# Flamingo block, one core: context projections of the second attention behind the experts, routing first on all engines, second attention reordered

## Chip, core and metric

One core of one Trainium2 chip. The engines are TensorE (PE in the profile), VectorE (DVE), ScalarE (ACT), GpSimd (POOL) and SyncE (SP, which issues the transfers). The metric is the device time of one execution in microseconds.

## What is computed

32 sequences of 64 tokens with 128 features go through two layers; each adds a gated attention over a context and a gated feed-forward part:

```python
x = x + tanh(g_xattn[0]) * attention(layernorm(x), ctx)       # softmax, 16 heads, rotary
x = x + tanh(g_ffn[0])   * experts(layernorm(x))              # 2 of 8 experts per sequence
x = x + tanh(g_xattn[1]) * autocorrelation(layernorm(x), ctx) # below
x = x + tanh(g_ffn[1])   * fp4_ffn(layernorm(x))              # gate/up 352 wide, SiLU, down
# autocorrelation, per sequence and head:
corr = irfft(rfft(Q) * conj(rfft(K))).mean(-1); w, idx = top_k(corr, 4); w = softmax(w)
out = sum_k w[k] * roll(V, idx[k]) @ Wo + bo
```

The router takes the mean of a sequence's tokens, picks the two best of eight logits, and weighs both experts' outputs with a softmax. `fp4_ffn` rounds its inputs and weights in blocks of 16 to an eight-value grid.

## The kernel before

Every engine has its own instruction list in an order written out by hand; semaphores (`m[...]`) join them, and each engine works its list strictly in order. The tokens are 16 tiles of 128 x 128 (two sequences each), in four groups. `ps` is PSUM with eight banks of 512 columns; a step may not overwrite a bank before its reader has gone.

- **First attention** (to about 99 us): 16 tiles, one after the other.
- **Routing** (99 to 120.4). `pool_tokens` (L1165) sums the normalised tokens on PE into bank 0, DVE copies them (`pooled`, L759), PE forms the logits (L1182), and DVE and PE take turns: best two, membership `mem`, ranks, `tcol`, `tend`, slots (L761 to L797). `experts` (L791) releases SP, whose `feed` copies each expert's weights from `wall` into one of six `wbuf`; `packed` (L806) releases POOL, whose `gather` (L380) copies the chosen sequences out of `xt`. Meanwhile PE turns the tokens (`turn_tokens`, L1034), takes the context to frequencies (`context_to_frequency`, L1143) and projects it (`context_kv`, L1159, eight steps of 512 columns: four for K, four for V). ACT copies each K and V step out of PSUM twice: plain (`kf`, `vf`, L532) and with real and imaginary halves exchanged (`kfs`, `vfs`, L534). DVE fills `acc` with the experts' second bias (L809, 2048 columns), adds biases to the zero frequency of K and V (L819), and PE waits for `acc_ready` ahead of the first expert.
- **Experts**: 36 tiles of two slots. `hidden(j)` (L1214), GELU on ACT (L542), `second(j)` (L1223), `collect` on DVE adds into `acc`. POOL also prepares the fp4 weights.
- **Second attention**: `turn_weights` (L1241, L1245) and its copies, then PE turns `acc` back (L1254), DVE adds it to `x` and takes statistics (`moe_out`), POOL raises to a power (`powers`), ACT normalises (L239). `to_frequency` (L1262), `queries` (L1269), a bias on DVE (L871), `products` with K (L874), `sum_heads` (L1283), `correlate` (L1293, L1299), `best_lags` (L880 to L896, with ACT's `exp_lead`), `turn_lags`, `turn_gx` (L581), `spectrum` (L1329), `roll_values` (L904), POOL's `values_added` (L408), `out_product` (L1336), `y1_turned`, `out_tokens` (L1343), and DVE's `attention_out` (L932) with `x_stats`.
- **fp4 part**: per group of four tiles `x_scale` (L265 to L272), `x_magnitude` on ACT, `x_round` (L276), `x_unscale` on POOL (L283), `turn_x` (L1369), `turned_x` (L614). Per pair of tiles `gate_up` (L1379), `silu` (L619) and `pair_step` on DVE, which begins with the product of L957, then `turn_h` and `down`. Groups 2 and 3 are scaled and rounded inside the loop over pairs.

## Time and profile before

| | us |
|---|---|
| median of 3 runs (311.04 to 312.18) | 312.07 |
| profiled execution | 312.27 |
| its span, first to last instruction | 310.5 |
| PE busy | 260.1 |
| DVE busy | 205.5 |
| ACT busy | 163.6 |
| POOL busy | 114.7 |
| mean granted clock of PE, 1 is full | 0.943 |

The span is what the trace shows; 1.77 us of the profiled execution lie around it. Busy time is an average over the stages above, and in each of them another engine or chain sets the end, so it is to be read by stretch. In a timeline, a number in brackets is the idle time of the engine ahead of the row, with what ended it; "x8" means eight instructions in a row.

### The profile page before, as it was taken

To read this page: it belongs to the slowest core of one execution; us is meant where nothing else is said; L and a number is where in the kernel's file an instruction comes from. 1 tells how busy PE (TensorE), PEld (TensorE's weight loads), DVE (VectorE), ACT (ScalarE), POOL (GpSimd) and SP (SyncE) were. 2 spreads that over 40 slices of the span, in tenths; PEclk is the share of its full clock that TensorE was granted. 3 is DMA by queue.
4 is the path that set the end of the run, shared out by engine and by line. 5 is a ranking of instruction groups with operands and counts; after the bars stand their busy time and mean duration, and the time that the engine had idled before them with its cause. 6 is when DMAs were issued, how large, how long until landed. Compare 5 with 4: busy or idle time off the path is not lost.

```text
span 310.5 us, 6172 instructions
## 1 busy us (share of the span) xinstructions
PE 260.1 (84%) x2126; PEld 199.1 (64%) x2126; DVE 205.5 (66%) x556; ACT 163.6 (53%) x381; POOL 114.7 (37%) x163
## 2 busy tenths in 40 slices
PE   2999889999898988999999994987892857598675
PEld 1565257666667935999999993666661424467474
DVE  3499988888986355342322337663989499999951
ACT  1169365666584578775566553762327352434321
POOL 3174549993202103229952202300554303231230
PEclk9999999999999999999999999699997588979957
DMA  7994000000000208676777710000000000001011
GB/s 246 357 387 196 0 3 2 2 2 0 3 2 2 74 2 364 262 303 276 292 291 305 291 70 3 1 0 2 0 0 1 0 2 0 0 17 34 19 34 35
DMA packets 11871, 30.13 MB, mean 97 GB/s; under 512 B 961, under 2 KB 5057, under 8 KB 11713
## 3 DMA queue, kind: packets, MB, share of 16 engines
q1 hardware_dynamic: 11840, 29.75, 25.2%
q8 instruction: 17, 0.28, 0.4%
q14 instruction: 14, 0.11, 0.1%
HBM read 9.75 MB, written 1.05 MB: 35 GB/s over the span
## 4 chain that ended last, share of the span: by engine, by line
PE 53%; DVE 30%; ACT 7%; issue 5%; DMA 3%; POOL 1%; SPq 0%; DVEq 0%
PE ps L1223 10%; PE ps L1214 9%; PE ps L1104 5%; DVE s_region L276 4%; PE ps L1078 4%; PE ps L1091 4%; DVE s_small L225 3%; DVE s_region L680 3%; PE ps L1401 2%; DVE s_small L967 2%; DVE s_region L272 2%; PE ps L1114 2%; PE ps L1283 2%; DMA s_region<-s_wall 2%; PE ps L1379 2%
## 5 line engine op out<-in xcount | busy, mean ns | idle before, releaser
L542 ACT ACTIVATE s_region<-ps,s_region 128x128 f32<-128x128 f32 x144 | 40.8, 371 | 20.5 <-PE ps L1214 20.4
L834 DVE SCALAR_TENSOR_TENSOR s_ctxT<-ps,s_region,s_ctxT 128x64 f32 x72 | 18.1, 281 | 45.7 <-PE ps L1223 45.4
L1214 PE MATMUL ps<-s_region 128*128 128x128 f32 x288 | 37.9, 276 | 0.8 <-DVE s_ctxT L810 0.5
L1223 PE MATMUL ps<-s_region 128*128 128x128 f32 x288 | 38.0, 276 | 0.5 <-ACT s_region L542 0.5
L1214 PEld LDWEIGHTS ps<-s_region 128*128 128x128 f32 x288 | 34.9, 192 | 1.8 <-DVE s_ctxT L810 1.3
L1223 PEld LDWEIGHTS ps<-s_region 128*128 128x128 f32 x288 | 35.0, 192 | 0.9 <-ACT s_region L542 0.7
L1379 PE MATMUL ps<-s_region 128*128 128x352 f32 x64 | 25.9, 558 | 11.3 <-DVE s_region L957 6.1
L283 POOL TENSOR_TENSOR s_region<-s_region,s_small 128x704 f32<-128x704 f32 (+2 forms) x13 | 17.5, 1343 | 47.6 <-DVE s_region L276 47.6
L248 POOL TENSOR_TENSOR s_small<-s_small,s_par 128x4 f32<-128x4 f32 (+3 forms) x14 | 15.5, 1108 | 47.1 <-DVE s_small L231 47.1
L380 POOL COPY s_region<-s_xt 128x64 f32 x72 | 14.9, 240 | 40.2 <-PE ps L1214 21.9
L490 ACT COPY s_region<-ps 128x512 f32<-128x512 f32 x32 | 17.2, 589 | 18.2 <-PE ps L1091 18.2
L1379 PEld LDWEIGHTS ps<-s_region 128*128 128x128 f32 x64 | 13.8, 227 | 20.2 <-issue 10.3
L338 POOL TENSOR_SCALAR s_region<-s_region 128x512 f32<-128x512 f32 x16 | 24.7, 1567 | 3.7 <-PE ps L1078 3.7
L701 DVE TENSOR_REDUCE s_small<-ps 128x16 f32<-128x1024 f32 x16 | 19.6, 1222 | 6.5 <-PE ps L1078 6.5
L239 ACT ACTIVATE s_xn<-s_x,s_small 128x128 f32<-128x128 f32 x48 | 19.9, 485 | 6.9 <-POOL s_small L250 6.8
L276 DVE SCALAR_TENSOR_TENSOR s_region<-s_region 128x704 f32<-128x704 f32 (+1 forms) x24 | 20.3, 848 | 2.2 <-ACT s_region L625 0.9
L1401 PE MATMUL ps<-s_region 128*128 128x128 f32 (+1 forms) x96 | 15.6, 324 | 5.9 <-DVE s_x L979 4.1
L1401 PEld LDWEIGHTS ps<-s_region 128*128 128x128 f32 (+1 forms) x96 | 14.6, 234 | 9.0 <-issue 5.9
L485 ACT ACTIVATE s_region<-s_region 128x1024 f32<-128x1024 f32 x16 | 17.1, 1069 | 6.2 <-DVE s_region L709 6.2
L709 DVE TENSOR_TENSOR s_region<-ps,s_small 128x1024 f32<-128x1024 f32 x16 | 18.7, 1171 | 0.1
L1104 PEld LDWEIGHTS ps<-s_region 128*64 128x64 f32 x512 | 16.3, 138 | 3.5 <-ACT s_region L490 1.9
L1104 PE MATMUL ps<-s_region 128*64 128x18 f32 x512 | 17.8, 212 | 0.7 <-ACT s_region L490 0.6
(205 smaller groups left out, 507.0 us busy)
## 6 DMA issues: line engine op xcount, KB each, us to landing
s_region<-s_wall SPq DMA_DIRECT2D x36, 514.0 KB, 3.2
s_wall<-wall SPq DMA_DIRECT2D x8, 514.0 KB, 9.2
s_par<-par SPq DMA_DIRECT2D x1, 1316.0 KB, 11.1
s_ctxT<-ctxT SPq DMA_DIRECT2D x2, 512.0 KB, 6.0
s_x<-x SPq DMA_DIRECT2D x2, 512.0 KB, 7.4
out<-s_x SPq DMA_DIRECT2D x8, 128.0 KB, 1.8
s_region<-ffn SPq DMA_DIRECT2D x1, 560.0 KB, 3.6
s_par<-par SPq DMA_DIRECT2D x1, 460.0 KB, 3.8
```

The lines of the kernel that those rows point to most:

```text
L239: ins = eng.activation(xn[:, t, :], x[:, t, :], ACT.Identity, bias=shift[:, t:t + 1], scale=rstd[:, t:t + 1])
L276: return eng.scalar_tensor_tensor(out, mag, 1.5, z, ALU.max, ALU.subtract)
L338: pool.tensor_scalar(kbd[g % 2][:, j, :], cols, hmask[:, j:j + 1], None, ALU.mult).then_inc(m["kbd_done"], 1)
L542: ins = act.activation(hg[j % 3][:, c, :], ps[:, j % 3, RPT * S * c:RPT * S * (c + 1)], ACT.Gelu, bias=wbuf[j % 6][:, FF + FC * D + c:FF + ...
L701: dve.tensor_reduce(mx[t % 2], scores(t % 2), AX, ALU.max).then_inc(m["mx_done"], 1)
L709: dve.tensor_tensor(ssub[t % 2], scores(t % 2), mx[t % 2].unsqueeze(2).broadcast_to([P, H, S]), ALU.subtract).then_inc(m["s_sub"], 1)
L834: dve.scalar_tensor_tensor(row, ps[:, 4 + j % 2, S * k:S * k + S], w, row, ALU.mult, ALU.add).then_inc(m["acc_done"], 1)
L1104: ins = mm(ps[S * row:S * row + S, 6 + t % 2, n * c:n * c + n], pT[t % 2][:, c, S * row:S * row + S], vbd[:, 2 * t + row, c, :], start=Tru ...
L1214: ins = mm(ps[:, j % 3, RPT * S * c:RPT * S * (c + 1)], w[:, P * c:P * c + P], xg[j % 4], start=True, stop=True)
L1223: ins = mm(ps[:, 4 + j % 2, 0:RPT * S], w[:, FF + D * c:FF + D * c + D], hg[j % 3][:, c, :], start=(c == 0), stop=(c == FC - 1))
L1379: ins = mm(ps[:, 1 + 2 * n + t % 2, 0:MLP], xqT[(t // 4) % 2][:, P * (t % 4):P * (t % 4) + P], wguT[:, MT * P * n:MT * P * n + MLP], start ...
L1401: ins = mm(ps[:, 7, D * t:D * t + D], hT[q % 2][0:n, t, k, :], wdT[0:n, k, :], start=(k == 0), stop=(k == MT - 1))
```

## The change

The exchanged copies `kfs` and `vfs` go; DVE reads `kf` and `vf` with the two halves in reverse order. The biases of Q, K and V are added on PE, by a product of the identity with eight columns of bias into the same bank (`frequency_bias`). During routing PE does routing steps ahead of everything else, and only `context_to_frequency(0)` to `(2)` stay ahead of the experts; `context_to_frequency(3)` and all eight `context_kv` move behind them, and so does `turn_weights`, to the middle of the second attention. ACT instead of DVE fills `acc`, POOL clears its spare rows at the start. The order of the second attention changes on every engine, the last two groups are normalised by DVE, `x_round(1)` moves into the loop over pairs, and the first `gate_up` waits for the value products, not for the last attention output. The core of the diff:

```diff
...
-        kf, kfs, vf, vfs = (carve(2048 * i, B, 2, DFT) for i in range(4))
+        kf, vf = carve(0, B, 2, DFT), carve(4096, B, 2, DFT)
...
+            for q in range(4):
+                values_added(q)
+            powers(pool, 0, 4)
+            values_added(4)
+            values_added(5)
             powers(pool, 4, 8)
+            values_added(6)
+            values_added(7)
+            x_unscale(0)
...
-            x_unscale(0)
...
+                if q in (2, 4):
+                    x_unscale(q // 2 + 1)
...
+                act.copy(ctxF[:, 512 * g:512 * g + 512], ps[:, 3 if g == 3 else 4 + g % 2, :]).then_inc(m["cf_used"], 1)
...
-            tokens_turned(0)
...
+                z, bank = (kf, 6 + n % 2) if n < G4 else (vf, 2 + n % 2)
+                act.copy(z[:, 8 * (n % G4):8 * (n % G4) + 8].rearrange("p b c s -> p (b c s)"), ps[:, bank, :]).then_inc(m["kv_used"], 1)
...
+            for g in range(3):
+                tokens_turned(g)
...
             act.activation(le[0:B], ld[0:B], ACT.Exp).then_inc(m["le_ready"], 1)
...
-                plain, swapped = (kf, kfs) if g < G4 else (vf, vfs)
-                src = ps[:, 6 + g % 2, :].rearrange("p (b c s) -> p b c s", c=2, s=DFT)
-                act.copy(plain[:, rows], src)
-                for c in range(2):
-                    ins = act.copy(swapped[:, rows, 1 - c], src[:, :, c])
-                ins.then_inc(m["kv_used"], 1)
+            tokens_turned(3)
+            context_turned(0)
+            context_turned(1)
+            context_turned(2)
+            act.wait_ge(m["b2_done"], 1)
+            act.copy(acc[:, 0:B, :], ps[:, 2, 0:B].unsqueeze(2).broadcast_to([P, B, S])).then_inc(m["acc_ready"], 1)
...
+            preload(ACT.Exp)
...
+            kv_turned(0)
+            context_turned(3)
+            kv_turned(1)
             normalise(act, 0, 4, m["xn_c"], 7)
+            kv_turned(2)
+            x_turned(0)
             normalise(act, 4, 8, m["xn_c"], 8)
-            x_turned(0)
-            normalise(act, 8, 12, m["xn_c"], 9)
+            kv_turned(3)
+            q_turned(0)
             x_turned(1)
-            q_turned(0)
-            normalise(act, 12, 16, m["xn_c"], 10)
             x_turned(2)
             q_turned(1)
...
             x_turned(3)
-            q_turned(2)
+            heads_turned(0)
             q_turned(3)
-            preload(ACT.Exp)
-            heads_turned(0)
             exp_lead(0)
             heads_turned(1)
+            kv_turned(4)
             turn_gx(0)
+            kv_turned(5)
             exp_lead(1)
+            preload(ACT.Silu)
...
+            kv_turned(6)
+            kv_turned(7)
+            weights_turned(0)
+            weights_turned(1)
             y1_turned(0)
+            weights_turned(2)
...
@@ -630,30 +640,27 @@
                     act.wait_ge(m["xd_done"], g - 1)
                 act.activation(qm[g % 2], qv[g % 2], ACT.Abs, scale=FINE).then_inc(m["xm_done"], 1)
 
...
-            normalise(act, 0, 4, m["xn_d"], 11)
-            y1_turned(3)
             normalise(act, 4, 8, m["xn_d"], 12)
             x_magnitude(0)
-            preload(ACT.Silu)
+            y1_turned(3)
+            turned_x(0)
             normalise(act, 8, 12, m["xn_d"], 13)
-            turned_x(0)
...
             x_magnitude(1)
-            silu(0)
             normalise(act, 12, 16, m["xn_d"], 14)
-            turned_x(1)
             for q in range(PAIRS + 1):
-                g = q // 2 + 2
...
-                if q in (2, 4):
+                if q in (0, 2, 4):
                     turned_x(q // 2 + 1)
 
...
-            normalise(dve, 8, 12, m["xn_b_late"], 4)
+                if t == 14:
+                    normalise(dve, 8, 12, m["xn_b_late"], 4)
...
-            sr.did(dve.tensor_copy(lidf[0:B], lidx[0:B, 0:2]))
-            sr.step(dve.tensor_tensor(ld[0:B], lmax[0:B, 1:2], lmax[0:B, 0:1], ALU.subtract))
-            dve.sem_inc(m["ld_ready"], 1)
+            sr.step(dve.tensor_copy(lidf[0:B], lidx[0:B, 0:2]))
             for k in range(2):
                 sr.did(dve.tensor_scalar(oh[0:B, k, :], pc("iota_e", B), lidf[0:B, k:k + 1], None, ALU.is_equal))
             sr.settle()
+            dve.tensor_tensor(mem[0:B], oh[0:B, 0, :], oh[0:B, 1, :], ALU.add).then_inc(m["route_in"], 1)
+            dve.tensor_tensor(ld[0:B], lmax[0:B, 1:2], lmax[0:B, 0:1], ALU.subtract).then_inc(m["ld_ready"], 1)
...
+            dve.tensor_tensor(ohb[0:B], ohs[0:B, 0, :], ohs[0:B, 1, :], ALU.add).then_inc(m["route_in"], 1)
...
-            dve.tensor_copy(acc[:, 0:B, :], ps[:, 2, 0:B].unsqueeze(2).broadcast_to([P, B, S])).then_inc(m["acc_ready"], 1)
...
+            sr.did(dve.tensor_scalar(wt[0:B], oh[0:B, 0, :], lw[0:B, 0:1], None, ALU.mult))
+            sr.step(dve.tensor_scalar(ohw[0:B], ohs[0:B, 0, :], lw[0:B, 0:1], None, ALU.mult))
+            dve.scalar_tensor_tensor(wt[0:B], oh[0:B, 1, :], lw[0:B, 1:2], wt[0:B], ALU.mult, ALU.add).then_inc(m["wt_ready"], 1)
+            dve.scalar_tensor_tensor(ohw[0:B], ohs[0:B, 1, :], lw[0:B, 1:2], ohw[0:B], ALU.mult, ALU.add).then_inc(m["wt_ready"], 1)
+            dve.wait_ge(m["wt_turned"], 1)
+            dve.tensor_copy(wtT[0:E], ps[0:E, 3, P:P + B]).then_inc(m["wt_copied"], 1)
+            dve.wait_ge(m["wt_turned"], 2)
+            dve.tensor_copy(wB, ps[:, 1, 0:SLOTS]).then_inc(m["weights_spread"], 1)
+            dve.wait_ge(m["weights_spread"], 1)
+            dve.wait_ge(m["spare_zero"], 2)
+            dve.wait_ge(m["acc_ready"], 1)
...
-                    dve.tensor_scalar(z[:, :, c, 0], z[:, :, c, 0], b64[:, 1 + n:2 + n], None, ALU.add).then_inc(m["kv_biased"], 1)
...
-                dc.step(dve.tensor_scalar(qf[:, rows, 0, 0], qf[:, rows, 0, 0], b64[:, 0:1], None, ALU.add))
...
+                for z, k in ((pp, kf[:, rows]), (pq, kf[:, rows, ::-1, :])):
+                    dve.tensor_tensor(z[:, rows], qf[:, rows], k, ALU.mult).then_inc(m["pp_done"], 1)
...
+                for z, (o, v) in enumerate(((of1, vf[:, rows]), (of2, vf[:, rows, ::-1, :]))):
...
+            normalise(dve, 8, 12, m["xn_c_late"], 9)
+            products(0)
+            normalise(dve, 12, 16, m["xn_c_late"], 10)
+            products(1)
             dve.tensor_scalar(bo1g, pc("bo1"), tg[:, 2:3], None, ALU.mult).then_inc(m["bo_scaled"], 1)
-            for g in range(G4):
-                products(g)
+            products(2)
+            products(3)
...
-                bias_added(q)
-            roll_values(4)
...
+            bias_added(0)
+            bias_added(1)
+            out_and_stats(0)
+            roll_values(4)
             roll_values(5)
-            out_and_stats(0)
+            out_and_stats(1)
+            x_scale(0)
             roll_values(6)
             roll_values(7)
-            out_and_stats(1)
+            x_round(0)
+            bias_added(2)
             out_and_stats(2)
-            x_scale(0)
-            attention_out(3)
-            x_round(0)
-            x_stats(3)
+            bias_added(3)
+            out_and_stats(3)
             x_scale(1)
-            x_round(1)
...
+                if q in (0, 2, 4):
+                    x_round(q // 2 + 1)
+                if q in (1, 3):
+                    x_scale((q + 3) // 2)
...
+                if t == TILES - 1:
+                    pool_tokens(0, 2)
                 weigh_values(t)
                 if t >= 1:
                     project_out(t - 1)
+            pool_tokens(2, 3)
             turn_output(TILES - 1)
+            pool_tokens(3, 4)
...
+            def frequency_bias(bank, n):
+
+                pe.wait_ge(m["bias64_ready"], 1)
+                out = ps[:, bank, :].rearrange("p (b c s) -> p b c s", c=2, s=DFT)[:, :, 0, 0]
+                return mm(out, ident, b64[:, n, :], start=False, stop=True)
...
+                pe.wait_ge(m["cf_used"], n + 1 if n < G4 else G4)
+                bank = 6 + n % 2 if n < G4 else 2 + n % 2
+                if n < 2:
+                    pe.wait_ge(m["tr2_used"], n + 3)
+                elif n < G4 or n >= G4 + 2:
                     pe.wait_ge(m["kv_used"], n - 1)
+                elif n == G4:
+                    pe.wait_ge(m["xf_used"], G4)
                 else:
-                    pe.wait_ge(m["tr2_used"], n + 3)
-                mm(ps[:, 6 + n % 2, :], pc("wk1" if n < G4 else "wv1"), ctxF[:, 512 * (n % G4):512 * (n % G4) + 512],
-                   start=True, stop=True).then_inc(m["kv_done"], 1)
-
...
+                mm(ps[:, bank, :], pc("wk1" if n < G4 else "wv1"), ctxF[:, 512 * (n % G4):512 * (n % G4) + 512], start=True, stop=False)
+                frequency_bias(bank, 1 + n // G4).then_inc(m["kv_done"], 1)
...
+            pool_tokens(4, 12)
...
+            pool_tokens(12, TILES).then_inc(m["pool_sums"], 1)
             pe.wait_ge(m["pooled_ready"], 1)
             mm(ps[0:B, 1, 0:E], pooled, pc("wr"), start=True, stop=True).then_inc(m["route_mm"], 1)
-            context_kv(0)
-            context_kv(1)
-            context_kv(2)
+            turn_tokens(1)
+            turn_tokens(2)
...
+            turn_tokens(3)
...
+            context_to_frequency(0)
...
+            context_to_frequency(1)
+            pe.wait_ge(m["wt_ready"], 1)
+            tr(ps[0:E, 3, P:P + B], wt[0:B], pc("ident", B)[:, 0:B]).then_inc(m["wt_turned"], 1)
+            pe.wait_ge(m["wt_ready"], 2)
+            mm(ps[:, 1, 0:SLOTS], pc("ones", B), ohw[0:B], start=True, stop=True).then_inc(m["wt_turned"], 1)
+            context_to_frequency(2)
+            pe.wait_ge(m["wt_copied"], 1)
+            mm(ps[:, 2, 0:B], pc("b2", E), wtT[0:E], start=True, stop=True).then_inc(m["b2_done"], 1)
...
+                elif j >= 1:
+                    pe.wait_ge(*((m["weights_spread"], 1) if j == 1 else (m["acc_ready"], 1)))
...
+                pe.wait_ge(m["wq_ready"], 1)
+                pe.wait_ge(*((m["wq_used"], 1) if g == 2 else (m["kv_used"], 7 + g)))
...
+                frequency_bias(2 * (g % 2) + 1, 0).then_inc(m["q_done"], 1)
...
+                pe.wait_ge(m["kv_used"], G4)
...
+            context_kv(0)
+            turn_experts(0)
+            turn_experts(1)
+            context_to_frequency(3)
+            context_kv(1)
+            turn_experts(2)
+            context_kv(2)
+            turn_experts(3)
             to_frequency(0)
+            context_kv(3)
+            queries(0)
             to_frequency(1)
-            queries(0)
             to_frequency(2)
             queries(1)
+            sum_heads(0)
+            queries(2)
             to_frequency(3)
-            queries(2)
-            sum_heads(0)
+            sum_heads(1)
             queries(3)
-            sum_heads(1)
             correlate(0)
             sum_heads(2)
             sum_heads(3)
+            context_kv(4)
...
             turn_lags(0)
             spectrum(0)
+            context_kv(5)
             spectrum(1)
             turn_lags(1)
             spectrum(2)
+            context_kv(6)
             spectrum(3)
+            context_kv(7)
+            turn_weights(0)
+            turn_weights(1)
             out_product(0)
+            turn_weights(2)
             spectrum(4)
+            spectrum(5)
             out_tokens(0)
-            spectrum(5)
             out_product(1)
+            out_tokens(1)
             spectrum(6)
-            out_tokens(1)
             spectrum(7)
-            for g in range(2, G4):
-                out_product(g)
-                out_tokens(g)
+            out_product(2)
+            out_tokens(2)
+            out_product(3)
+            out_tokens(3)
...
+                    pe.wait_ge(m["of_done"], 2 * PAIRS)
+                    pe.wait_ge(m["wq_used"], 3)
+                    if t == 1:
+                        pe.wait_ge(m["y1_ready"], G4)
...
+                else:
+                    pe.wait_ge(m["x3_done"], G4)
...
-            turn_x(1)
...
-                if q in (2, 4):
+                if q in (0, 2, 4):
                     turn_x(q // 2 + 1)
...
```

## Rows read from the trace of the kernel before

**Rows 1.** Busy time by stretch (us, then PE, PEld, DVE, ACT, POOL, PEclk, DMA).
```profile
99.00:120.40 21.40, 18.96 (x117) 12.53 (x115) 12.00 (x58) 12.85 (x31) 2.50 (x7) 1.00 0.26 96
120.40:186.70 66.30, 65.35 (x578) 64.84 (x579) 20.39 (x78) 43.99 (x150) 29.14 (x76) 1.00 0.66 266
186.70:199.00 12.30, 8.07 (x42) 6.39 (x41) 9.34 (x47) 7.25 (x17) 4.75 (x8) 0.75 0.00 1
```

**Rows 2.** Timeline of DVE, 101 to 120: start, us, line, operation, idle before.
```profile
101.74 1.29 DVE L241 TENSOR_SCALAR s_xn<-s_x,s_small 128x128 f32<-128x128 f32 x4
106.59 0.19 DVE L759 COPY s_small<-ps 128x32 f32<-128x32 f32 x1 [3.56 <-PE ps L1165]
108.18 0.15 DVE L761 TENSOR_SCALAR s_small<-ps 32x8 f32<-32x8 f32 x1 [1.40 <-PE ps L1182]
...
112.12 0.15 DVE L779 COPY s_small<-ps 32x8 f32<-32x8 f32 x1 [1.45 <-PE ps L1190]
...
114.36 0.18 DVE L791 TENSOR_SCALAR s_small<-ps 1x36 int32<-1x36 f32 x1 [0.56 <-PE ps L1196]
...
116.55 0.22 DVE L799 SCALAR_TENSOR_TENSOR s_small<-ps,s_par 1x72 f32<-1x72 f32 x1 [0.93 <-PE ps L1201]
...
117.93 2.27 DVE L809 COPY s_ctxT<-ps 128x2048 f32<-128x2048 f32 x1
```

**Rows 3.** Timeline of PE, 99 to 113.
```profile
99.92 1.85 PE L1165 MATMUL ps<-s_par,s_xn 128*128 128x2 f32 x16
...
110.67 1.10 PE L1159 MATMUL ps<-s_region,s_par 128*128 128x512 f32 x2 [0.46 <-ACT s_region L534]
```

**Rows 4.** Timeline of ACT, 121 to 127.
```profile
121.17 1.28 ACT L437 ACT_TABLE_LOAD   x1
...
122.70 4.42 ACT L542 ACTIVATE s_region<-ps,s_region 128x128 f32<-128x128 f32 x16
```

**Rows 5.** Timeline of POOL, 102 to 120.
```profile
119.49 0.24 POOL L380 COPY s_region<-s_xt 128x64 f32 x1 [16.85 <-issue]
```

**Rows 6.** Timeline of PE, from the end of the experts.
```profile
186.51 0.82 PE L1241 MATMUL ps<-s_par,s_region 128*128 128x128 f32 x6
...
187.95 1.04 PE L1254 MATMUL ps<-s_par,s_ctxT 128*128 128x128 f32 x8
...
194.13 2.08 PE L1262 MATMUL ps<-s_par,s_xn 128*128 128x128 f32 x8 [1.76 <-ACT s_xn L239]
...
242.66 5.00 PE L1379 MATMUL ps<-s_region 128*128 128x352 f32 x8 [0.67 <-ACT s_region L614]
...
249.53 2.60 PE L1379 MATMUL ps<-s_region 128*128 128x352 f32 x8 [1.42 <-DVE s_region L957]
...
270.13 3.88 PE L1379 MATMUL ps<-s_region 128*128 128x352 f32 x8 [3.56 <-ACT s_region L614]
```

**Rows 7.** Timeline of ACT, 218 to 224.
```profile
222.74 1.01 ACT L581 COPY s_region<-ps 128x1024 f32<-128x1024 f32 x1 [4.64 <-PE ps L1329]
```

**Rows 8.** Timeline of DVE, 219 to 287.
```profile
219.39 0.75 DVE L904 TENSOR_TENSOR s_region<-ps,s_region 128x256 f32<-128x256 f32 x2
...
227.44 0.74 DVE L932 SCALAR_TENSOR_TENSOR s_x<-ps,s_small,s_x 128x512 f32<-128x512 f32 x1
...
229.68 1.47 DVE L904 TENSOR_TENSOR s_region<-ps,s_region 128x256 f32<-128x256 f32 x4
...
235.55 0.68 DVE L265 TENSOR_REDUCE s_small<-s_xn 128x32 f32<-128x512 f32 x1
...
238.26 1.42 DVE L276 SCALAR_TENSOR_TENSOR s_region<-s_region 128x512 f32<-128x512 f32 x2
...
248.49 0.89 DVE L957 TENSOR_TENSOR s_region<-s_region,ps 128x704 f32<-128x704 f32 x1 [3.30 <-ACT s_region L619]
...
280.63 0.88 DVE L957 TENSOR_TENSOR s_region<-s_region,ps 128x704 f32<-128x704 f32 x1
...
286.23 0.89 DVE L957 TENSOR_TENSOR s_region<-s_region,ps 128x704 f32<-128x704 f32 x1
```

183 lines of the change are left out of this document (64 added, 119 removed).

## Prediction

> **What bounds the kernel now.** I read the page first, then busy time by stretch, then each engine's timeline around the stretches that the change touches. Four limits follow each other. From 99 to 120.4 no engine is full: PE, ACT and DVE pass the routing result back and forth, with context work queued between the steps [rows 1]. From 120.4 to 186.7 PE is busy 65.35 of 66.30 us [rows 1]: the experts are PE's, nothing is gained inside them, and what counts is when they start. From 186.7 PE waits for DVE's statistics and its granted clock averages 0.75 [rows 1], half speed at 194 [rows 6]. From about 219 DVE sets the pace: its groups carry no idle time except 3.30 us before the first product of the pair loop at 248.49 [rows 8]; later one pair step takes 286.23 - 280.63 = 5.60 us [rows 8].
>
> Times below are on the clock of the trace of before. The sum is made against the profiled execution, 312.27 us (span 310.5 and 1.77 around it), 0.2 above the median of 312.07.
>
> **Part 1: routing first.** Before, the last token tiles are normalised from 101.74 to 103.03 [rows 2] and their sums reach DVE at 106.59, behind two `context_to_frequency` and two `turn_tokens`. Now `normalise(dve, 8, 12)` runs in DVE's idle time in tile 14, so the last tile is ready about 1.0 earlier, at 102.05; four of the sixteen pooled tiles go into attention's gaps (a tile costs 1.85 / 8 = 0.23 of PE [rows 3]), and one is left when the last normalise ends. The sums are read at 102.5, 4.1 earlier.
> - L759 to L761: 1.59 [rows 2], of it 1.40 waiting for PE behind context work; now about 0.5. Gain so far 5.2.
> - L761 to L779: 3.94, with 1.45 of waiting behind `context_kv(2)` and the softmax weights in line. Now 1.4 of arithmetic to `mem` and 0.35 for two small matmuls: 104.7, gain 7.4.
> - L779 to L791: 2.24; the wait of 0.56 behind `context_kv(3)` and the copy of `wtT` go: 106.3, gain 8.1. `experts_ready` and the weight transfers move with it.
> - L791 to L799: 2.19; two operations on `ohw` and most of the 0.93 wait go: 107.45, gain 9.1.
> The codes are packed 1.3 later (108.8), and POOL's first row copy, at 119.49 before [rows 5], comes at 110.4. Expert 0's first matmuls can start at 111.2.
>
> Then ACT is late. It still has `context_turned(2)` (PE work of 0.9 queued ahead of the `b2` product, ends 111.45), then the broadcast into `acc`, formerly DVE's 2.27 [rows 2]. A broadcast copy of 1024 columns takes ACT 1.01 [rows 7]; 2048 columns I take at 1.9, to 113.4. The GELU table costs 122.70 - 121.17 = 1.53 [rows 4]: first GELU at 115.0 against 122.70. **Gain 7.7.** Behind ACT's new wait for `b2_done` stand the GELUs; PE's `hidden(1)` and `hidden(2)` wait for `weights_spread` (110.3) and `acc_ready` (113.4), both before `second(0)` could run. POOL's wait for `tr2_used` ends at 105.9, long before the codes. No transfer changes its place on SP. Low 6.2, if each of the eight hand-offs costs 0.2 more than I read; high 8.9, if the `acc` copy finished as early as the rest of the routing. The swapped copies on ACT and four bias additions on DVE lay in front of this point and are inside the gain.
> The Trainium skill (ScalarE: Activation LUTs, What ACT_TABLE_LOAD costs) puts every switch of tables at about 2.66 us, a drain behind the load included. This trace does not agree: the load lasts 1.28 and the next instructions follow at once [rows 4]; by the page the gain would be 6.6.
>
> **Part 2: front of the second attention.** After the experts the three turned weights (1.44 from 186.51 to 187.95 [rows 6]) give way to `context_kv(0)`: 512 columns, issue to issue 0.86 (a pair shows 1.10 with its tail [rows 3]), and a bias matmul of about 0.21. So the statistics start 0.4 earlier. The other context work, `context_to_frequency(3)` 0.9 and two `context_kv` 1.07 each, fills PE while it waited, so the clock should not fall at 193. A mean of 0.75 means that half of the 12.3 us were at half clock [rows 1]; eight 128-wide instructions take 1.04 at full and 2.08 at half [rows 6], so some 5.3 us of PE work from 194.1 shrink by 2.7. ACT's `preload(Exp)`, 1.5, leaves the path too. Against it stand `context_kv(3)` and `(4)`, 2.1, and four bias products, 0.8. I take the second correlation 2.0 earlier. Then the new order gives it back: ACT does `kv_turned(5)` before `exp_lead(1)`, and `context_kv(5)` stands behind `spectrum(0)` on PE. `exp_lead(1)` is ready at 215.7 and runs at 218.6, 2.9 late; DVE waits for it. `roll_values(0)` starts at 220.0 instead of 219.39 [rows 8].
>
> **Part 3: the output chain.** `spectrum(3)` has `context_kv(6)` in front, so `turn_gx(1)` starts at 223.85, before 222.74 [rows 7]. From there everything is in line: 1.0 for it; `kv_turned(6)` and `(7)` 1.1; then `turn_weights(1)` 0.35, `out_product(0)` 0.9, `turn_weights(2)` 0.35, `spectrum(4)` and `(5)` 1.7, `out_tokens(0)` 1.1: 230.4. DVE adds the first group at 230.4, before at 227.44 [rows 8]: **3.0 late**, with some 4.7 of DVE idle.
>
> DVE's queue to the pair loop, by rows 8: four outputs with statistics at 229.68 - 227.44 = 2.24; four value products at 1.38 / 2 (from 1.47 for two pairs); two scalings at 238.26 - 235.55 - 0.78 = 1.93; one rounding 1.34; two bias additions taken at 0.65 (below the 0.74 of an output of the same columns); 0.35 of waiting for ACT. Sum 8.96 + 2.76 + 3.86 + 1.34 + 1.30 + 0.35 = 18.6: first product of the pair loop at 249.0, against 248.49. The 3.30 that DVE idled there is thus what pays for the late output. `gate_up(0)` and `(1)` start at about 244.8; they took 5.00 at half clock, 2.60 for the next two at full clock [rows 6]. The first product followed the gates' start by 5.83 [rows 6, 8], so 0.83 goes to SiLU and hand-offs: 248.2 or 250.6, and the loop starts at 249.0 or 250.6. PE has gaps of up to 2.4 shortly before; I take 249.6: **1.1 lost** (0.5 to 2.1).
>
> **Part 4: the pair loop.** `x_round(1)` moves into it: **1.3 lost**. X tiles arrive one step later than before. From the end of a rounding, 239.68, to the first product made of it, 248.49, passed 8.8 at half clock [rows 8], 6.4 with gates at 2.60. After rounding 1 and 2 a step and a scaling, 7.4, cover it roughly; after rounding 3 one step of 5.6 alone. Half clock is likely there: the pair of gates at 270.13 came after 3.56 of idle and took 3.88 [rows 6]. That makes 7.6, and 2.0 late; full clock 0.8. **I take 1.2**, bounds 0 and 3.2.
>
> **Sum.** 312.27 - 7.7 + 1.1 + 1.3 + 1.2 = 308.2, less 0.2 for the median: **308.0**. Nearly half of the gain in routing is given back. Operands read with the halves reversed: no row has one; DVE's products are costed as plain ones (256 columns 0.37 [rows 8]), and the other bound, twice that, adds 3 over eight value products. I take nothing, since the runs of 32 numbers stay whole. The new memset on POOL stands before its first waits for DVE.
>
> **Rivals.**
> - **A, all of the gain stays (304 to 306.4).** Clock full at the first gates, no late tile, and the 2.0 of Part 2 kept in part: 312.1 - 7.7 + 0.5 + 1.3 = 306.2, less up to 2. For it: the 3.30 of idle. Against it: the order on ACT in Part 2. Chance 0.22.
> - **B, the pair loop waits at each new X tile (310.5 to 313.5).** Gates at 5.00 throughout: start at 250.6 (2.1), rounding 1.3, late by 0.8, 0.9 and 3.2: 8.3 lost, 312.7. For it: rows 6 show 5.00 and 3.88. Against: most groups of the loop start after short waits. Chance 0.15.
> - **C, half clock between 214 and 230 (above 313.5; slower).** PE's work on the path there, two spectra, three `context_kv`, turned weights, `out_product(0)`, `out_tokens(0)`, sums to about 8.4 at full clock and would double; all of Part 3 is in line, so `out_tokens(0)` ends near 238, and 308.0 becomes 316. It decides once 5 us of that PE work run at half clock. For it: the stop and go with ACT. Against: PE's gaps there are 1.5 at most, and 194.13 was at half clock after a longer quiet stretch [rows 6]. Chance 0.13.
> The Trainium skill (TensorE: Matmul & The Clock Gate, HAM oscillation) warns of this pattern: each wait that lets the clock fall makes the next group run cold, again and again. By it C gains weight; what rows 6 show at 194, 242 and 270 agrees.
> - **D, routing's head start does not reach the experts.** Weights arrive late or ACT's chain grows, and only 5 of 7.7 remain: 310.7. Against: the transfers are issued 8 earlier too. It overlaps B's times; chance 0.05.
> The forecast itself, 306.4 to 310.5, has 0.45.
>
> **Numbers.** A measurement of this kernel tells about 0.5%, 1.6 us, from no change. Faster by more: the forecast, A and 0.03 of D: 0.70; within: B and 0.02 of D, 0.17; slower: C, 0.13. The range takes in the forecast, nearly all of A, D and most of B, some 0.83: 304.5 to 312.5.
>
> **What would show it.** First GELU near 115.0, with `experts_ready` 8 earlier; PE's clock 1.0 between 187 and 200; ACT's exponent of the second half near 210.9 (218.6 less 7.7) with DVE waiting; first attention output near 222.7; first pair product near 242; a gap before the seventh. Wrong if the GELU gain is under 6, or if DVE does not idle before the first output.

## The result: slower, 317.9 us against 311.8

| | before | after |
|---|---|---|
| median of four runs each (lowest to highest), us | 311.81 (311.04 to 312.18) | 317.90 (316.69 to 319.68) |
| profiled execution, us | 312.27 | 318.17 |
| its span | 310.5 | 316.4 |
| mean granted clock of PE in it | 0.943 | 0.905 |

The ratio of after to before is 1.0176, 95% interval 1.0131 to 1.0222. Ratios, here and below, leave out the slower executions that some kernels have now and then, while medians are over all. Forecast were 308.0, with 304.5 to 312.5 as range. Read by way points, as lengths between them in the two profiled executions, the 5.9 us of the span lie so (the first is where the last tile of the first attention weighs its values on PE; the forecast column is worked out from the prediction's own clock times):

| stretch | before | after | difference | forecast |
|---|---|---|---|---|
| start to last attention tile | 96.22 | 95.63 | -0.59 | 0 |
| to the first GELU | 26.48 | 23.89 | -2.59 | -7.7 |
| experts, to DVE's first group added | 65.96 | 65.38 | -0.58 | 0 |
| to the first value product | 30.73 | 31.69 | +0.96 | +0.6 (with the row above) |
| to the first attention output | 8.05 | 10.63 | +2.58 | +2.4 |
| to the first product of the pair loop | 21.05 | 22.27 | +1.22 | -1.9 |
| to its last, eighth | 43.31 | 48.32 | +5.01 | +2.5 (with the row below) |
| to the end | 18.70 | 18.59 | -0.11 | |

The gain in routing is 5.1 smaller than forecast, the start of the pair loop 3.1 later, the loop 2.4 longer; the other rows came out within 0.6.

First the busy time by stretch of the changed kernel; the first three lines answer to [rows 1], the last two cut the first stretch in two.

```profile
99.00:120.40 21.40, 20.75 (x102) 18.43 (x102) 8.00 (x47) 8.41 (x15) 4.26 (x16) 0.52 0.45 175
120.40:186.70 66.30, 66.22 (x577) 64.78 (x576) 21.99 (x83) 43.61 (x147) 27.24 (x67) 1.00 0.59 240
186.70:199.00 12.30, 10.69 (x68) 8.13 (x67) 11.43 (x51) 7.59 (x17) 5.78 (x8) 1.00 0.01 2
...
99.00:109.00 10.00, 9.37 (x52) 8.35 (x52) 5.44 (x33) 2.44 (x5) 1.74 (x4) 0.51 0.18 57
109.00:120.40 11.40, 11.38 (x52) 10.08 (x52) 2.56 (x15) 5.97 (x10) 2.52 (x12) 0.53 0.69 278
```

The column after POOL is the granted clock. After the experts it went from 0.75 to 1.00, as forecast. In routing it went from 1.00 to 0.52, and that the prediction had not priced. PE had *less* work of routing there than before (the context projections are gone) and yet shows 20.75 us busy of 21.40, against 18.96. Part of that is the first experts' products, which now begin at 116.00; the rest is the same work at half speed.

PE's timeline of the changed kernel (line numbers are now its own: L1123 sums, L1156 context to frequency, L1365 output matmul, L1411 gates). Answers to [rows 3] and [rows 6].

```profile
98.44 2.67 PE L1123 MATMUL ps<-s_par,s_xn 128*128 128x2 f32 x16
...
101.86 1.71 PE L1123 MATMUL ps<-s_par,s_xn 128*128 128x2 f32 x8
...
113.43 2.08 PE L1156 MATMUL ps<-s_par,s_ctxN 128*128 128x128 f32 x8
...
190.38 1.16 PE L1273 MATMUL ps<-s_par,s_xn 128*128 128x128 f32 x8 [1.31 <-ACT s_xn L239]
...
237.27 1.16 PE L1358 MATMUL ps<-s_par,s_region 128*128 128x128 f32 x8 [1.95 <-POOL s_region L408]
...
240.03 2.05 PE L1365 MATMUL ps<-s_region,s_par 128*128 128x512 f32 x2 [1.60 <-DVE s_x L932]
...
243.60 5.06 PE L1411 MATMUL ps<-s_region 128*128 128x352 f32 x8 [0.68 <-ACT s_region L624]
250.52 5.03 PE L1411 MATMUL ps<-s_region 128*128 128x352 f32 x8 [1.86 <-DVE s_region L957]
...
264.77 5.03 PE L1411 MATMUL ps<-s_region 128*128 128x352 f32 x8 [3.37 <-DVE s_region L957]
...
287.51 4.05 PE L1411 MATMUL ps<-s_region 128*128 128x352 f32 x8 [0.68 <-ACT s_region L624]
```

Sixteen instructions of sums (the products of two columns that sum the tokens, two instructions each) took 1.85 before [rows 3] and take 2.67; a context group of eight takes 2.08, the half-speed duration of [rows 6]. Later the last output matmul (2.05, the three before it 1.1) and four of eight pairs of gates are slow (5.06, 5.03, 5.03, 4.05). Before it was three: 5.00 and 3.88 [rows 6], and one of 4.05. Two gaps of PE, 1.95 and 1.60 us, lie just ahead of the fall; the clock is 1.00 up to 238 and 0.50 from 240 on.

DVE's timeline, for [rows 2] and [rows 8]:

```profile
103.60 0.19 DVE L767 COPY s_small<-ps 128x32 f32<-128x32 f32 x1 [2.27 <-PE ps L1123]
108.49 0.18 DVE L794 TENSOR_SCALAR s_small<-ps 1x36 int32<-1x36 f32 x1
...
110.69 0.22 DVE L801 SCALAR_TENSOR_TENSOR s_small<-ps,s_par 1x72 f32<-1x72 f32 x1 [1.36 <-PE ps L1207]
...
215.53 0.29 DVE L889 SCALAR_TENSOR_TENSOR s_region<-s_region 128x128 f32<-128x128 f32 x1 [2.68 <-ACT s_region L574]
...
227.22 0.75 DVE L932 SCALAR_TENSOR_TENSOR s_x<-ps,s_small,s_x 128x512 f32<-128x512 f32 x1 [4.09 <-PE ps L1365]
...
249.49 0.89 DVE L957 TENSOR_TENSOR s_region<-s_region,ps 128x704 f32<-128x704 f32 x1 [3.03 <-ACT s_region L629]
...
256.38 0.89 DVE L957 TENSOR_TENSOR s_region<-s_region,ps 128x704 f32<-128x704 f32 x1 [2.15 <-ACT s_region L629]
...
292.38 0.89 DVE L957 TENSOR_TENSOR s_region<-s_region,ps 128x704 f32<-128x704 f32 x1 [1.69 <-ACT s_region L629]
```

The waits that the prediction named are there: 2.68 for ACT's second exponent, 4.09 ahead of the first output. The wait of 1.36 at L801 was 0.93 before [rows 2] and was to go for the most part: `context_to_frequency(0)` stands in front of the small matmul and takes 2.08 at half clock, where the prediction took 0.9 for such a group. Inside the pair loop DVE waits twice for the SiLU behind slow gates, 2.15 and 1.69; in the kernel before it has no idle time inside the loop.

ACT, for [rows 4] and [rows 7]:

```profile
115.54 0.59 ACT L514 COPY s_region<-ps 128x512 f32<-128x512 f32 x1 [2.33 <-PE ps L1156]
116.10 1.87 ACT L534 COPY s_ctxT<-ps 128x2048 f32<-128x2048 f32 x1
117.98 1.28 ACT L441 ACT_TABLE_LOAD   x1
...
119.52 4.43 ACT L541 ACTIVATE s_region<-ps,s_region 128x128 f32<-128x128 f32 x16
...
214.63 0.59 ACT L523 COPY s_region<-ps 128x512 f32<-128x512 f32 x1 [2.20 <-PE ps L1171]
215.11 0.31 ACT L574 ACTIVATE s_region<-s_region 128x128 f32<-128x128 f32 x1
```

The broadcast of 2048 columns took 1.87 (taken at 1.9), the table switch 117.98 to 119.52 = 1.54 (before 1.53). ACT's last context copy came at 115.54, its matmuls having ended late: that is the 4.5 us by which the GELU (119.52, forecast 115.0) is late. POOL's first row copy, at 119.49 before [rows 5], came at 114.07 (forecast 110.4):

```profile
114.07 0.87 POOL L382 COPY s_region<-s_xt 128x64 f32 x4 [13.12 <-issue]
```

### The profile page after: what moved, and what is told of

It is laid out like the page before. It is cut to its first block, busy times and chain, and to the rows that moved or that the text cites. A ratio compares the mean times of both kernels' runs of the same rounds, so it can differ in the third digit from the quotient of the medians.

```text
span 316.4 us, 6202 instructions
## 1 busy us (share of the span) xinstructions
PE 272.1 (86%) x2150; PEld 209.7 (66%) x2150; DVE 204.7 (65%) x554; ACT 157.7 (50%) x358; POOL 115.2 (36%) x164
## 4 chain that ended last, share of the span: by engine, by line
PE 63%; DVE 23%; ACT 5%; issue 5%; DMA 2%; POOL 1%; SPq 0%; DVEq 0%; ACTq 0%; POOLq 0%
PE ps L1227 11%; PE ps L1236 10%; PE ps L1411 6%; PE ps L1107 5%; PE ps L1081 4%; PE ps L1094 4%; DVE s_small L225 3%; DVE s_region L687 3%; PE ps L1435 2%; DVE s_region L276 2%; PE ps L1295 2%; PE ps L1156 2%; PE ps L1117 2%; DVE s_region L957 2%; PE ps L1351 2%
## 5 line engine op out<-in xcount | busy, mean ns | idle before, releaser
L1227 PE MATMUL ps<-s_region 128*128 128x128 f32 x288 | 39.7, 284 | 0.1
L1236 PE MATMUL ps<-s_region 128*128 128x128 f32 x288 | 38.1, 276 | 0.0
L1411 PE MATMUL ps<-s_region 128*128 128x352 f32 x64 | 29.6, 623 | 9.8 <-DVE s_region L957 6.5
L1227 PEld LDWEIGHTS ps<-s_region 128*128 128x128 f32 x288 | 36.6, 200 | 0.4 <-issue 0.2
L1236 PEld LDWEIGHTS ps<-s_region 128*128 128x128 f32 x288 | 35.0, 192 | 0.4 <-ACT s_region L541 0.2
L1411 PEld LDWEIGHTS ps<-s_region 128*128 128x128 f32 x64 | 15.5, 255 | 20.8 <-issue 13.5
L708 DVE TENSOR_REDUCE s_small<-ps 128x16 f32<-128x1024 f32 x16 | 19.6, 1224 | 6.5 <-PE ps L1081 6.5
L276 DVE SCALAR_TENSOR_TENSOR s_region<-s_region 128x704 f32<-128x704 f32 (+1 forms) x24 | 20.5, 855 | 1.7 <-ACT s_region L635 0.9
L239 ACT ACTIVATE s_xn<-s_x,s_small 128x128 f32<-128x128 f32 x40 | 16.6, 487 | 5.8 <-POOL s_small L250 5.8
L629 ACT ACTIVATE s_region<-ps 128x704 f32<-128x704 f32 x8 | 6.1, 758 | 25.8 <-PE ps L1411 25.8
L1094 PE MATMUL ps<-s_par,s_region 128*128 128x128 f32 x128 | 16.7, 273 | 2.0 <-ACT s_region L489 2.0
```

Of the source, the lines that this page charges most:

```text
L276: return eng.scalar_tensor_tensor(out, mag, 1.5, z, ALU.max, ALU.subtract)
L708: dve.tensor_reduce(mx[t % 2], scores(t % 2), AX, ALU.max).then_inc(m["mx_done"], 1)
L1094: ins = tr(ps[:, 4 + half, P * k:P * k + P], pr[t % 2][:, c:c + P], ident)
L1227: ins = mm(ps[:, j % 3, RPT * S * c:RPT * S * (c + 1)], w[:, P * c:P * c + P], xg[j % 4], start=True, stop=True)
L1236: ins = mm(ps[:, 4 + j % 2, 0:RPT * S], w[:, FF + D * c:FF + D * c + D], hg[j % 3][:, c, :], start=(c == 0), stop=(c == FC - 1))
L1411: ins = mm(ps[:, 1 + 2 * n + t % 2, 0:MLP], xqT[(t // 4) % 2][:, P * (t % 4):P * (t % 4) + P], wguT[:, MT * P * n:MT * P * n + MLP], start ...
```

## The experiments

Fourteen kernels. Way points as above, in each one's profiled execution; A is the last attention tile's start, so that the later columns don't hold what happened before routing. A column's difference between two kernels is one between two single executions, and some stretches take a different time in different executions of the same code (last section). The ratio is to runs of before on the same chip.

| kernel | A | to GELU | to group added | to value product | to output | to pair product | to eighth | to end | median | ratio (95%) |
|---|---|---|---|---|---|---|---|---|---|---|
| before | 96.22 | 26.48 | 65.96 | 30.73 | 8.05 | 21.05 | 43.31 | 18.70 | 311.8 | 1 |
| after | 95.63 | 23.89 | 65.38 | 31.69 | 10.63 | 22.27 | 48.32 | 18.59 | 317.9 | 1.018 (1.013, 1.022) |
| e1 | 95.50 | 21.93 | 65.38 | 31.68 | 10.63 | 21.95 | 46.63 | 18.70 | 315.0 | 1.011 (1.004, 1.017) |
| e2 | 95.70 | 19.02 | 67.01 | 31.69 | 10.64 | 22.26 | 47.54 | 18.64 | 315.6 | 1.011 (1.005, 1.017) |
| e3 | 95.60 | 26.06 | 67.01 | 31.68 | 10.64 | 22.25 | 47.68 | 18.58 | 320.8 | 1.023 (1.017, 1.030) |
| e4 | 98.24 | 23.02 | 65.37 | 31.68 | 11.30 | 20.35 | 43.26 | 18.58 | 312.6 | 0.996 (0.992, 1.000) |
| e5 | 98.26 | 19.01 | 67.01 | 31.69 | 11.30 | 21.11 | 44.11 | 16.41 | 310.1 | 0.991 (0.988, 0.995) |
| e6 | 98.79 | 19.01 | 67.01 | 29.04 | 11.89 | 21.02 | 43.28 | 18.66 | 309.9 | 0.991 (0.988, 0.994) |
| e7 | 95.62 | 31.41 | 65.77 | 31.62 | 8.24 | 21.04 | 43.30 | 18.60 | 317.5 | 1.015 (1.011, 1.019) |
| e8 | 96.13 | 19.03 | 65.95 | 31.70 | 11.30 | 19.78 | 44.11 | 18.70 | 309.9 | 0.992 (0.988, 0.996) |
| e9 | 95.88 | 19.81 | 65.35 | 33.21 | 10.64 | 24.11 | 44.69 | 16.41 | 312.1 | 1.001 (0.998, 1.004) |
| e10 | 96.33 | 19.55 | 65.65 | 32.97 | 10.63 | 28.34 | 45.93 | 17.90 | 319.0 | 1.023 (1.020, 1.027) |
| e11 | 96.99 | 20.50 | 65.41 | 29.04 | 11.89 | 19.78 | 43.29 | 22.10 | 312.0 | 1.001 (0.997, 1.004) |
| e12 | 97.50 | 27.60 | 65.79 | 29.85 | 8.04 | 19.78 | 43.31 | 22.03 | 317.5 | 1.016 (1.012, 1.020) |
| e13 | 96.55 | 19.02 | 65.37 | 31.70 | 10.63 | 19.08 | 46.14 | 18.61 | 312.0 | none |
| e14 | 95.57 | 19.02 | 67.50 | 29.05 | 11.89 | 18.23 | 43.27 | 17.97 | 304.9 | 0.978 (0.974, 0.982) |

### Why the clock fell in routing: e1, e2, e3, e7

**e1** puts two context groups back among the sums:

```diff
+            context_to_frequency(0)
             pool_tokens(4, 12)
             turn_tokens(0)
+            context_to_frequency(1)
             pool_tokens(12, TILES).then_inc(m["pool_sums"], 1)
```

> The changed kernel, with context_to_frequency(0) put ahead of the token sums of tiles 4 to 11 on PE and context_to_frequency(1) ahead of those of tiles 12 to 15; nothing else differs. Theory K (the two-column sums that now stand alone let PE's clock fall at 99.4): with 128-column work among them the granted clock stays at 1.0 through routing, the first GELU comes at 116.5 to 118 instead of 119.5, and the whole falls by 1.5 to 3 us. Rival Q (the clock falls because PE waits for the other engines during routing, whatever it did before): clock 0.5 as before from about 100, the first GELU 0 to 2 us later than 119.5 because 1.8 us of PE work stand ahead of the sums, time unchanged or up to 2 us longer.

**e2** gives the token sums of twelve of the sixteen tiles all 128 columns of the same constant, and DVE reads out the same two of each, with one small copy more:

```diff
-                    ins = mm(ps[:, 0, 2 * t:2 * t + 2], xn[:, t, :], pc("dft")[:, 0:P:S], ...)
+                    if t < 4: ...
+                    else:
+                        ins = mm(ps[:, 1 + t // 4, P * (t % 4):P * (t % 4) + P], xn[:, t, :], pc("dft"), ...)
```

> The changed kernel with the same token sums for tiles 4 to 15, in the same places and with the same weights, but 128 columns wide instead of 2 (DVE then picks the columns it wants, one small copy more). Theory K (few columns, not idle time, let the clock fall): the clock stays at 1.0 past 99.4, at least to the small matmuls of routing, the first GELU comes 1.5 to 3 us sooner than 119.5 and the time falls by as much. Rival Q: the clock falls at about 99.4 as before, the first GELU at 119.5 to 121, time up by 0 to 1.5 us.

**e3** leaves the sums narrow and adds eight idle 128-column matmuls: one ahead of the sums of every two of tiles 4 to 11, one behind `turn_tokens(0)`, and three among the turns and small matmuls that follow:

> The changed kernel with eight 128-column products of constants, read by nobody, put into PE's list: one ahead of every second tile's sums for tiles 4 to 11, one after turn_tokens(0), and one in each of the next three waits of routing. They add 1.8 us of PE work at full clock, most of it where PE waits. Theory K: clock 1.0 through routing, first GELU at 115.5 to 117.5, whole time 2 to 4 us shorter. Rival Q or a rival in which the clock does not matter here: first GELU at 119.5 to 121.

**e7** goes the other way, in the kernel before: its three context groups that lie among the sums go behind them, and ACT's copies follow that order.

```diff
-            context_to_frequency(0)
             pool_tokens(0, 8)
             ...
-            context_to_frequency(1)
...
-            pool_tokens(8, 15)
-            turn_tokens(2)
-            context_to_frequency(2)
-            pool_tokens(15, TILES).then_inc(m["pool_sums"], 1)
-            context_to_frequency(3)
+            pool_tokens(8, TILES).then_inc(m["pool_sums"], 1)
+            turn_tokens(2)
+            for g in range(G4):
+                context_to_frequency(g)
```

> The kernel before with one edit: the three context products that lay among the token sums go behind them, on PE and ACT, so that the 2-column sums run with only token turns between them; nothing is left out. Theory K (a stretch of 2-column matmuls with little wide work among it lets the granted clock fall): the granted clock falls to 0.5 at some point between 100 and 107 and stays there for a good part of the routing; the sums are read by DVE at most 1.5 earlier than before's 106.59, and the first GELU comes at 124 to 128 against 122.70; ratio 1.00 to 1.02. Rival M (the clock fell in the changed kernel for some other reason than the missing context work, such as the order of the last attention tiles): clock 1.00 throughout 99 to 120, sums read near 104.5, first GELU 121 to 123, ratio 0.995 to 1.00.

Busy time by stretch of e7, and then PE's timeline of it:

```profile
99.00:109.00 10.00, 10.00 (x50) 10.00 (x50) 3.40 (x15) 1.79 (x4) 2.03 (x4) 0.50 0.19 57
109.00:120.40 11.40, 9.85 (x55) 5.56 (x54) 4.41 (x29) 8.17 (x20) 0.00 (x0) 0.99 0.01 1
```
```profile
98.42 2.82 PE L1163 MATMUL ps<-s_par,s_xn 128*128 128x2 f32 x16
...
102.85 3.41 PE L1163 MATMUL ps<-s_par,s_xn 128*128 128x2 f32 x16
```

The old kernel, with only the wide work between its sums taken out, lost the clock at once (0.50 from 99 to 109), and its GELU came at 127.03, inside the 124 to 128 of the theory; counted from the last attention tile it is 4.9 later. Rival M falls: the order of the last tiles or anything else new in the changed kernel isn't needed for the fall. (The 4.9 hold the new order of the context work too, not the clock alone.) The same stretches and PE rows in e2:

```profile
99.00:109.00 10.00, 7.96 (x68) 6.59 (x66) 7.46 (x47) 3.50 (x7) 1.74 (x4) 1.00 0.24 87
109.00:120.40 11.40, 9.64 (x62) 8.94 (x63) 1.15 (x6) 7.96 (x20) 3.43 (x16) 0.85 0.74 300
```
```profile
98.51 1.95 PE L1127 MATMUL ps<-s_par,s_xn 128*128 128x128 f32 x16
```

Sixteen instructions of 64 times the columns took 1.95, shorter than the narrow ones at half speed (2.67). The granted clock held through the sums, and the GELU came at 114.72, 4.8 earlier than in the changed kernel, more than the 1.5 to 3 expected. The way to it is 19.02, 7.5 shorter than before (19.0 in five more kernels with wide sums, and 19.6, 19.8 and 20.5 in e10, e9 and e11, which lost the clock for a part of the way). Not all of it reaches the end of the experts: in e2 the clock is 0.56 to 0.59 from 116 to 120, right behind the first GELU, and the experts' stretch takes 67.01, 1.6 more than in the changed kernel (65.38). e3, e5 and e6 show the same 67.01 and e14 67.50, while e13, with the same code up to there as e2, kept 1.00 and took 65.37. e1 held the clock through the sums (1.84 for sixteen) and lost it from about 106 on: 21.93, between the two; its GELU at 117.43 and its 2.9 us less than the changed kernel are as Theory K said, but the clock did not stay up to the end of routing. e3 is a miss. Its idle matmuls, in pairs of instructions, did not hold the clock, which fell near 99 all the same, and each cost its own time; the GELU came at 121.66, later than both theories had it:

```profile
99.00 0.71 PE L1152 MATMUL ps<-s_par 128*128 128x128 f32 x2
99.50 0.85 PE L1123 MATMUL ps<-s_par,s_xn 128*128 128x2 f32 x4
```

Shown is what went ahead of the fall: after narrow sums with nothing or little wide between them (the changed kernel, e7, e3) the clock fell, and with wide sums (e2) or a whole context group ahead of each run of narrow ones (e1) it stayed at 1.00 through the sums. Why e3's idle matmuls did not do what e1's groups did is open. The Trainium skill (TensorE: Matmul & The Clock Gate, Why this matters for your kernels) names padding as one cure for thin matmuls under which the clock swings. Its case is one with waits for transfers between the bursts; here the narrow sums ran one behind the other, and in e2 padding kept the clock too. The same page (What's actually happening) says that the gate goes by how busy PE has been. The busy share of the profile can't be read as that: it was 10.00 of 10.00 in e7 with the clock at 0.50.

### Where the tail lost: e4, e9, e10, e13

**e4** restores, in the changed kernel, the old order of the output chain and of the pair loop on all engines (`spectrum(5)` behind `out_tokens(0)` on PE; on DVE the bias additions among the first value products, the second and third output in a row; `x_round(1)` and `turn_x(1)` ahead of the loop).

> The changed kernel with the order of before from the value products on: on DVE the value products and outputs, x_scale and x_round before the pair loop and the last two groups in steps 0 to 3 of it, and the matching lists of PE, ACT and POOL; routing and the moved context work stay as changed. Theory T (the late X tiles and the rounding moved into the loop cost what Part 4 of the prediction says and more, 4.9 us between the first product of the pair loop and the end): that distance falls from 66.9 to about 62 us and the whole time by 2 to 5 us. Rival (the loop is long only because the clock is low in this execution): the distance stays within 1 us of 66.9.

The distance came out as Theory T said: from the first pair product to the end 61.84, before 62.01, after 66.91. Since the output chain and the loop went back together, it does not tell which of them cost it. In its routing the clock was back at 1.00 from 116 on, in the changed kernel's from 120 on; the 0.9 less to the GELU is not the edit's. **e9** is e2 with only the loop in the old order:

```diff
             x_scale(1)
+            x_round(1)
             for q in range(PAIRS + 3):
                 pair_step(q)
-                if q in (0, 2, 4):
-                    x_round(q // 2 + 1)
...
```

> The changed kernel with wide sums, and of the tail only the loop over pairs as before: second X tile rounded and turned ahead of the loop, groups 2 and 3 scaled and rounded in the old steps; the new output chain stays. Theory S (the loop's new schedule of the X tiles costs 5 us: first pair product to the end took 66.9 and 66.2 with it, 60.5 to 62.0 without it): 61 to 62.5 us from the first pair product to the end, first pair product 1.0 to 1.5 later than with wide sums alone (the rounding is in front again), so the span is 3 to 4 shorter. Rival O (the slow loop comes from the output chain, which lets the clock fall before the gates, and the loop only inherits it): 65 us or more from the first pair product to the end, span the same or longer.

From the first pair product to the end it took 61.10, as Theory S said. But 2.2 of that is the last stretch (16.41), where the clock came back sooner (e5 has the same 16.41 with the same loop, e4 and e6 have 18.6). The loop from first to eighth product became 2.85 shorter, and the rounding that now stands in front cost 1.85. The schedule of the loop alone thus costs about 1.0 net, not the 5. The span is 2.4 shorter than e2's where 3 to 4 were expected: from 209 to 213 the clock was down in e9, and the way to the first value product took 1.5 more (1.3 in e10). **e10** is e2 with sixteen idle matmuls of 256 columns before `turn_x(0)`:

> The changed kernel with wide sums and its new tail, and sixteen idle 256-column matmuls before the first turn of the fp4 tokens. Theory S (the loop's length is the new schedule: an X tile arrives late after each rounding) with half clock only adding to it: the gates take 2.6, the first pair product comes 1 to 2.5 earlier, from there to the end still 64.5 us or more. Rival H (the long loop is half clock and nothing else): with the gates warm the loop falls to 62 to 63.5 from the first pair product to the end, and the span is 4 us or more shorter than with wide sums alone.

Inconclusive as meant, since the clock had fallen at about 237, before the idle work began. Each idle matmul is two instructions and takes 0.44 at full speed; sixteen take 7.07 there (e8), not some 4, and here they took 9.12, so the pair loop began 6 us later. From its first product to the end 63.83 passed, between the 62 to 63.5 of Rival H and the 64.5 of Theory S. **e13** puts smaller ones (0.25 each) inside the two gaps ahead of the fall instead:

```diff
             out_tokens(2)
+            idle_work(6)
             out_product(3)
+            idle_work(5)
             out_tokens(3)
```

> The changed kernel with wide sums and its new tail, and idle 128-column matmuls in PE's two gaps there: six in the 1.94 us before the last output product, five in the 1.60 us before the last output matmul (each takes about 0.24). Theory (the new output chain costs 3 us at the start of the pair loop because its gaps let the clock fall before the last output matmul, 2.05 at half clock where the others take 1.1, and the gates take 5.06): clock 1.0 up to the gates, gates 2.6, first attention output to first pair product 19 to 20 where it was 22.3, and the loop no more than 1 us shorter, since its X tiles come late by the schedule. Rival H (everything after the first output that is slow in the new tail is half clock): the loop from first to last pair product 44.5 or less, where it was 47.5. Rival F (the clock falls a few us later in exchange): first pair product within 1 us of before the edit.

```profile
231.21 1.50 PE L1345 MATMUL ps<-s_par 128*128 128x128 f32 x12
233.33 1.16 PE L1366 MATMUL ps<-s_par,s_region 128*128 128x128 f32 x8 [0.62 <-POOL s_region L408]
234.32 1.28 PE L1345 MATMUL ps<-s_par 128*128 128x128 f32 x10
236.09 1.10 PE L1373 MATMUL ps<-s_region,s_par 128*128 128x512 f32 x2 [0.48 <-DVE s_x L933]
...
238.29 2.63 PE L1421 MATMUL ps<-s_region 128*128 128x352 f32 x8 [0.68 <-ACT s_region L624]
...
243.37 4.28 PE L1421 MATMUL ps<-s_region 128*128 128x352 f32 x8 [2.44 <-DVE s_region L958]
```
```profile
248.48 0.89 DVE L958 TENSOR_TENSOR s_region<-s_region,ps 128x704 f32<-128x704 f32 x1 [1.39 <-ACT s_region L629]
...
283.06 0.89 DVE L958 TENSOR_TENSOR s_region<-s_region,ps 128x704 f32<-128x704 f32 x1 [0.27 <-ACT s_region L629]
```

Output matmul 1.10, gates 2.63, and the stretch from first output to first pair product 19.08 in place of e2's 22.26: 3.2 us were half clock, brought on by the two gaps (1.94 and 1.60 in e2). DVE no longer waits ahead of its first pair product (3.03 in the changed kernel). Rival H falls, since the loop keeps 46.14 against 43.3 in the old order; rival F too, though the second pair of gates is at 4.28. The second fence is DVE's, the only two waits that it has inside this loop: 1.66 together, where the changed kernel has 2.15 + 1.69 = 3.84. Taken off, both loops are 44.48 long. The runs lie in two pairs (309.1 and 309.6; 314.4 and 314.6, with mean clocks 0.97 and 0.94), so no ratio is given; what the second pair lost is not known, and the readings above are of the 309.1.

### Together: e5, e6, e8, e11, e12, e14

**e5** is e2 and e4 in one.

> The changed kernel with both edits tried singly: twelve of the sixteen token sums as full 128-column matmuls, and the output chain and pair loop in the order of the kernel before; nothing is left out. Theory (two independent losses, K: the 2-column sums let the granted clock fall in routing; T: the new tail order costs at its end): the gains add. Wide sums gave a first GELU at 114.7 where the changed kernel had 119.5, the old tail 61.8 us from the first pair product to the end where the new one had 66.9. So: granted clock 1.0 up to 115, first GELU 115 to 116, first attention output 224 to 225, first pair product 244 to 245.5, span 305.5 to 307.5, profiled time 307.5 to 309.5, ratio to before 0.985. Rival (the early routing's gain is eaten by a fixed wait later, so only the tail counts): span as with the old tail alone, 311 to 312, ratio 0.996 to 1.0. Rival (the clock that stays up in routing is lost again in the second half): first GELU 115 but the span from there to the end longer by over 3 us than in the run with the old tail alone.

Both gains are there, 19.01 to the GELU and 60.52 from first pair product to the end. The span of 308.9 is above the 305.5 to 307.5 of the theory, because the first attention lost the clock for about 5 us in this execution:

```profile
41.36 1.90 PE L1107 MATMUL ps<-s_region 128*64 128x18 f32 x32
43.19 1.97 PE L1094 MATMUL ps<-s_par,s_region 128*128 128x128 f32 x8
```

(1.11 and 1.09 in others.) It did so in three of the sixteen profiled executions (e4, e5 and e6, A of 98.2 to 98.8; elsewhere 95.5 to 97.5), in code that none of these three changed. Without it e5's span would be some 306.3, by the A of e2.

**e6** is e5 with `exp_lead(1)` ahead of `kv_turned(5)` on ACT.

> The kernel with wide sums and old tail, and one edit more: ACT takes the exponent of the second half of the lags ahead of the copy of the sixth context projection, not behind it. Theory (the prediction's Part 2: the exponent stands 2.9 us late behind that copy and its matmul, and DVE waits): DVE's idle of 2.7 before the second half's weights goes, the first value product and the first attention output come 2 to 3 us earlier, and the span is 1.5 to 3 shorter than with wide sums and old tail alone; the output chain may give back up to 1.5 because PE's next projection now waits for the copy. Rival (the wait only moves: the copy comes late, PE's projections behind it come late, and the first attention output stays): first value product up to 2 earlier but first output within 0.5 and span within 1 us.

ACT's and DVE's timelines of e6:

```profile
212.26 0.31 ACT L573 ACTIVATE s_region<-s_region 128x128 f32<-128x128 f32 x1
214.54 0.59 ACT L522 COPY s_region<-ps 128x512 f32<-128x512 f32 x1 [1.97 <-PE ps L1174]
```
```profile
213.85 0.75 DVE L905 TENSOR_TENSOR s_region<-ps,s_region 128x256 f32<-128x256 f32 x2
```

The exponent no longer waits for the copy, and the first value product comes 2.65 earlier (31.69 to 29.04). 0.6 is given back before the output, and the pair loop starts 2.1 earlier. The span, expected 1.5 to 3 shorter, is only 0.2 shorter: in e5's profiled execution one down product behind the loop ran at half clock (16.41 to the end), in e6's two (18.66). The median is the same as e5's; whether for the same reason, no trace shows.

**e8** is e5 with the sixteen idle matmuls of e10.

> The kernel with wide sums and old tail, and sixteen idle 256-column matmuls on PE between the last attention output and the first turn of the fp4 tokens, into columns that nobody reads (some 4 us of work in a gap of 5.1). Theory (half clock at the first gates costs time at the start of the pair loop): the eight gate matmuls take 2.6 in place of 4.3, the first pair product comes 1.0 to 2.0 earlier, and the span is 0.5 to 2 shorter. Rival 1 (fillers don't bring the clock up in time, as in the routing filler run): gates stay over 4.0, first pair product within 0.5 or later. Rival 2 (DVE's own work sets the loop's start): gates at 2.6 but the first pair product within 0.5.

The first gates took 2.63, and the first pair product came 1.3 earlier (19.78), though the idle work, 7.07 us in a gap of 5.1, ran over it. The median stayed at e5's (309.9 against 310.1); the end took 18.70. **e11** is e6 with idle work at three places, and **e12** is the kernel before with the same: fourteen of 128 columns before the first attention tile, the sixteen, and in the loop

```diff
                 if q >= 2:
                     down(q - 2)
+                for _ in range(20 if q == 7 else 6 if q == 8 else 0):
+                    mm(ps[:, 0, 0:P], ident, pc("dft"), start=True, stop=True)
```

> The kernel with wide sums, the old tail and the exponent first, and idle matmuls in three gaps of PE: fourteen of 128 columns before the first tile of the first attention, sixteen of 256 before the fp4 tokens, twenty and six of 128 between the last products of the loop. Theory (each stretch of half clock on the path costs its own time: 2.5 at the first attention in the executions where it comes, 2.3 at the first gates, 2.3 at the end): span 304 to 306, time 305.5 to 308, the spread of the runs narrower than the 3 to 5 us of the kernels without, ratio 0.98. Rival (the clock falls elsewhere in exchange, as in the run with warm gates, whose loop end took 18.7 where the other's took 16.4): median within 1 us of 309.9.

> The kernel before with the same idle matmuls in the same three gaps. Theory (the idle matmuls and the early routing are worth their time independently): the first gates at full clock and the end at full clock, 2 to 4.5 us faster than before, ratio 0.986 to 0.994, and 2 to 3 us slower than the kernel with everything. Rival (the clock falls elsewhere in exchange): ratio 0.996 to 1.003.

Both miss, although the mean clock of their profiled executions is high (0.982 and 0.971): faster was expected, and e11 is no faster than before and e12 slower. PE of e12 shows why:

```profile
295.96 2.90 PE L1403 MATMUL ps<-s_region 128*128 128x128 f32 x12 [3.35 <-DVE s_x L979]
298.65 4.85 PE L1419 MATMUL ps<-s_par 128*128 128x128 f32 x40
```

The end's idle work stood behind the down product, not in the gap of 3.35 ahead of it, and pushed the last turns and products back: 22.03 from the eighth product to the end, where it was 18.70. In e12 the attention also lost 1.3 and the way to the GELU 1.1, with half clock at about 84 and 115, which the kernel before doesn't have in its trace; the gates gained their 1.3, and the front of the second attention 0.9. The idle work at the start is the only edit ahead of 84, but as the attention's clock differs between executions of the same code, it is not shown to be the cause. **e14** is e6 with eight matmuls of 256 columns before `turn_x(0)` and ten of 128 ahead of `down(5)`.

> The kernel with wide sums, old tail and exponent first, and idle matmuls cut to what the gaps hold: eight of 256 columns (3.5 us, from 0.44 each) in the 5.1 us before the fp4 tokens, ten of 128 columns (2.4 us) in the 3.3 us before the sixth down product, none at the start. Theory (each gap filled within its length keeps its stretch at full clock and delays nothing): first output to first pair product 19.8, last pair product to the end 16 to 16.5, median 307 to 308.5, ratio 0.983 to 0.988. Rival (the clock falls elsewhere in exchange): first pair product 1.3 earlier but median within 1 of the kernel without idle matmuls, ratio 0.989 to 0.994.

```profile
231.17 3.62 PE L1441 MATMUL ps<-s_par 128*128 128x256 f32 x16
236.47 0.66 PE L1400 MATMUL ps<-s_par,s_region 128*128 128x128 f32 x4 [1.68 <-POOL s_region L283]
237.80 2.63 PE L1413 MATMUL ps<-s_region 128*128 128x352 f32 x8 [0.68 <-ACT s_region L623]
...
285.12 2.40 PE L1451 MATMUL ps<-s_par 128*128 128x128 f32 x20
288.62 1.57 PE L1437 MATMUL ps<-s_region 128*128 128x128 f32 x12 [1.11 <-DVE s_x L983]
```

304.9 us (303.1 to 306.4), ratio 0.978 (0.974 to 0.982), better than expected and the fastest of all. Here the idle work ended before its gap did (1.68 and 1.11 are left) and delayed nothing. Against e6 it is worth 2.8 at the start of the pair loop (1.2 expected) and 0.7 at the end (2.2 to 2.7 expected). The rest of the 6.2 between the two spans is not its doing: 3.2 are the first attention, which lost the clock in e6's execution and not in this one, and the experts took 0.5 more. At the end the next down product, at 293.40, took 2.55, so it ran mostly at half clock again. One pair of gates in the loop still took 5.03; the loop has the same 43.27 as e6's.

## Why the prediction was wrong

- **Part 1, sum of routing: the step that failed.** The GELU came 3.2 earlier by the clock of the trace (122.70 to 119.52), under the 6 that the prediction set as a sign of being wrong. Every duration in it was read at full clock, from a stretch whose clock the prediction itself quotes as 1.00 [rows 1]. It took away the wide context work and kept the 2-column sums, and did not ask what the clock rested on. With the clock held (e2) the order is worth 26.48 - 19.02 = 7.5, forecast 7.7. Hand-offs together, the broadcast on ACT and the table switch were sized well. The half clock cost 23.89 - 19.02 = 4.9 on the way to the GELU.
- **Part 2.** Right: clock 1.00 between 187 and 199, the second exponent behind `kv_turned(5)`. e6 measures that wait at 2.65, forecast 2.9. The front came out 0.4 longer with the experts' stretch taken in, forecast 0.6.
- **Part 3.** The late output was +2.6 behind the first value product, forecast 2.4. The start of the pair loop is the second failure. The prediction weighed 248.2 against 250.6 for the gates at full or half clock, named gaps of up to 2.4 ahead of them, and took 249.6 between the two, without a term for the output matmul and turns that run at half clock ahead of the gates. The value taken puts that start 21.05 - 1.9 = 19.15 after the first output; it was 22.27, and 19.08 with the two gaps filled (e13). The difference is the clock, 3.2: against e13 the gates start 1.4 later after the first output (16.38 against 15.02) and the product follows them 1.8 later (5.89 against 4.06). DVE's queue, which sets the start in e13, was sized well: 18.6 forecast, 19.08.
- **Part 4, the third.** Without DVE's waits the loop is 44.48 in the changed kernel and in e13, against 43.31 before, where DVE has none: the rounding moved into it costs 1.2, forecast 1.3. The waits are the term that was too small: 1.2 was taken, with 3.2 as bound, and they came to 3.84 in the changed kernel and 1.66 in e13. The 2.2 between these two go with slower gates inside the loop, 5.03, 5.03 and 4.05 against e13's 4.28 and 4.12. In the old order two slow pairs inside the loop (4.05 and 3.88) cost DVE no wait at all. That the first gap in the loop makes the next gates slow is read from the rows, not tried by itself.
- Together 4.9 + 3.2 + 2.2 = 10.3 us of half clock, against a miss of 10.0 (from -4.1 to +5.9), as a sum of differences between single executions. The first two are shown by an edit (e2, with e7 the other way, and e13); the last is read from DVE's waits. **Rival C** had the kind right (half clock, slower, over 313.5) and the place wrong: from 214 to 230 the clock was 1.00, and it fell before and after; that its time, 316, comes nearest is luck. Rival B had the gates at 5.00 but none of the routing.
- Operands with reversed halves cost nothing: two products of DVE with K took 1.28 in the changed kernel and 1.29 before (of the two, one reads reversed), and two value products of 256 columns 0.76, before 0.75.

## What to carry to other kernels

Work that filled PE between narrow matmuls was here also what held its clock; whoever moves it away must size every PE instruction that stays at both clock levels, and ask for each gap that the new order opens which matmuls run next. A full PE row in the profile is no sign that the clock holds. Where small matmuls must stand together, try wide moving operands (here 1.95 us for sixteen instructions where narrow ones took 1.84), and set idle matmuls only inside a measured gap, shorter than it and ahead of the waiting instruction. Compare single executions stretch by stretch: in two traces of the same code a stretch can differ by more than the edit is worth.

## What was not expected of the hardware

- 2-column matmuls with PE busy 10.00 us of 10.00 went with a granted clock of 0.50, the 1.2 GHz level (e7). Sixteen of 128 columns took 1.95 at the 2.4 GHz level, and sixteen of 2 columns 1.84 (e1) at the same level.
- The first attention loses the clock in some executions and not in others with the same code, worth 2.6 to 3.2 us (e4, e5 and e6 against the changed kernel, e2 and e14); so do the experts right behind the first GELU, 65.4 or 67.0, the stretch ahead of the first value product, 31.7 or 33.2, and the end of the loop, 16.41 or 18.6. Much of the spread of 3 to 5 us between a kernel's runs may come from such places; a time's mean clock goes with it in e13 (0.97 and 0.94), but not always (e6 has 307.8 at 0.936 and 310.0 at 0.942).
- An idle fp32 matmul is two instructions in the trace; one of 256 columns took 0.44 to 0.45 us (e8, e14) and one of 128 columns 0.24 to 0.26 (e14, e13), at the 2.4 GHz level.
